# Attention with half-row score products and four score banks

## The reference, cut to what matters

```
q = (seq2 + b_self) @ Wq + bq          # 128 x 128, as 16 heads of 8
k = concat(seq1 + b_prev, seq2 + b_self) @ Wk + bk
v = concat(seq1, seq2) @ Wv + bv
score_prev = einsum('bhqd,bhkd->bhqk', q, k[:, :, :l1]) * SCALE
score_self = (q * k[:, :, l1:]).sum(-1) * SCALE
weights = softmax(concat(where(mask, score_prev, -inf), score_self))
attn = weights[..., :-1] @ v[:, :, :l1] + weights[..., -1:] * v[:, :, l1:]
out = attn @ Wo + bo
```

## Time and profile before

| what | value |
|---|---|
| time, median of 3 runs | 452.58 us (448.89 to 454.62) |
| span of the profiled execution | 429.2 us |
| attention's steps with scores (i = 2 to 17) | 10.0 to 158.4 us of the span |
| PE busy share of the span | 87% |
| DVE, ACT, POOL | 65%, 58%, 46% |
| TensorE's granted clock, mean | 0.942 of full |

### The profile page before, as it was taken

The page is one execution under the profiler, slowest core; times in us unless marked ns, Lnnn a source line. Parts: engine busy times, 40 slices in busy tenths (PEclk is TensorE's granted clock), DMA queues, the critical chain, the costliest instruction groups (busy, mean ns, idle before and its releaser), DMA issues.

```text
span 429.2 us, 10202 instructions
## 1 busy us (share of the span) xinstructions
PE 375.2 (87%) x2637; PEld 270.4 (63%) x2637; DVE 278.9 (65%) x1132; ACT 247.4 (58%) x743; POOL 197.5 (46%) x273
## 2 busy tenths in 40 slices
PE   4999999899999995799998998479988779899960
PEld 4456556556666652689998997145565457677650
DVE  4566888888878888376555666369566536365562
ACT  2688788788887891546555564328874124344420
POOL 5421254444334434544554555223737506466561
PEclk9999999999999996599999999569999999899995
DMA  7603999678888404467767675320101122232354
GB/s 150 95 15 97 391 279 251 165 166 199 195 204 182 89 20 136 113 160 180 215 165 199 173 175 155 106 94 21 57 26 52 48 52 72 69 79 76 81 172 147
DMA packets 61072, 57.14 MB, mean 133 GB/s; under 512 B 6042, under 2 KB 49703, under 8 KB 60768
## 3 DMA queue, kind: packets, MB, share of 16 engines
q1 hardware_dynamic: 56288, 48.10, 45.1%
q0 software_dynamic: 4736, 8.47, 5.8%
HBM read 36.12 MB, written 21.73 MB: 135 GB/s over the span
## 4 chain that ended last, share of the span: by engine, by line
PE 58%; issue 12%; DMA 9%; DVE 8%; POOL 6%; ACT 4%; SPq 1%; POOLq 1%; DVEq 0%; ACTq 0%
PE bank L764 13%; PE bank L773 6%; PE bank L896 5%; PE bank L787 5%; PE bank L901 5%; DMA layer_outputs<-w_all 3%; POOL layer_outputs L744 3%; PE bank L1023 3%; DMA w_all<-layer_rows 2%; POOL layer_outputs L702 2%; PE bank L1103 2%; DMA qexp<-layer_outputs 2%; PE bank L804 2%; PE bank L818 2%; PE bank L871 2%
## 5 line engine op out<-in xcount | busy, mean ns | idle before, releaser
L1151 ACT ACTIVATE ps<-bank,ntop 128x128 f32<-128x128 f32 x256 | 73.4, 378 | 11.8 <-DVE ntop L1414 10.1
L1218 ACT ACTIVATE hT<-bank,w 128x128 f32<-128x128 f32 x176 | 50.8, 368 | 40.4 <-PE bank L896 40.1
L764 PE MATMUL bank<-qexp 128*128 128x512 f32 x128 | 67.8, 612 | 0.5 <-ACT ps L1151 0.5
L744 POOL DMA_INDIRECT layer_outputs<-w_all x40 | 39.9, 997 | 39.1 <-DVE w_all L1917 21.7
L773 PEld LDWEIGHTS bank<-ident,ps 128*128 128x128 f32 x256 | 31.9, 141 | 33.3 <-issue 29.8
L896 PE MATMUL bank<-xT,w 128*128 128x128 f32 x352 | 49.1, 284 | 2.8 <-DMA w<-in_L_ffn_w_dram 1.2
L1160 ACT ACTIVATE pT<-bank 128x512 f32<-128x512 f32 x64 | 38.6, 603 | 19.1 <-PE bank L773 18.1
L1413 DVE TENSOR_REDUCE mx<-bank 128x4 f32<-128x512 f32 x64 | 43.7, 683 | 8.5 <-PE bank L764 7.0
L668 POOL TENSOR_TENSOR qexp<-kA,rowmask 128x512 f32<-128x512 f32 x15 | 15.6, 1037 | 69.1 <-DVE kA L1498 69.1
L896 PEld LDWEIGHTS bank<-xT,w 128*128 128x128 f32 x352 | 44.6, 199 | 4.0 <-issue 2.6
L732 POOL DMA_INDIRECT layer_rows<-rows_all,places x32 | 30.8, 961 | 24.7 <-DVE rows_all L1791 10.3
(11 more groups left out here) (328 smaller groups left out, 814.6 us busy)
## 6 DMA issues: line engine op xcount, KB each, us to landing
w<-in_L_ffn_w_dram SPq DMA_DIRECT2D x44, 258.0 KB, 3.4
layer_rows<-fill SPq DMA_DIRECT2D x10, 910.0 KB, 9.1
w_all<-in_L_ffn_w_dram SPq DMA_DIRECT2D x24, 256.0 KB, 4.7
qexp<-layer_outputs SPq DMA_DIRECT2D x8, 512.0 KB, 4.0
xt<-layer_rows SPq DMA_DIRECT2D x45, 65.0 KB
w_all<-layer_rows SPq DMA_DIRECT2D x40, 65.0 KB, 1.9
xfT<-in_xfT_dram SPq DMA_DIRECT2D x16, 128.0 KB, 2.4
layer_rows<-fill SPq DMA_DIRECT2D x1, 1560.0 KB, 12.3
```

Source lines behind the costliest of these rows:

```text
L744: g.indirect_dma_start(ys1_dram, bass.IndirectOffsetOnAxis(ap=xt1[r][:, P:P + 1].bitcast(U32), axis=0), yb1[r][:, :], None, bounds_check=Y ...
L764: pe.matmul(psA[g % 2][:, :], qexp[b % 2][:, g, :], kexp[b % 2].rearrange("p g k -> p (g k)"), start=True, stop=True).then_inc(a_in_ps, 1)
L1151: m = s.activation(ps[g % 2][:, t, :], psA[g % 2][:, t * P:(t + 1) * P], ACT.Exp, bias=ntop[:, h:h + 1])
L1218: s.activation(hT[r % 2][:, c, :], banks[c][:, 0:P], ACT.Gelu, bias=w1[r][:, F0 + c:F0 + c + 1]).then_inc(gelu_done, 1)
```

## The change

- A head's eight rows of q and k now lie so that the groups' rows fall into halves: `rowmask` (four columns) is folded into `halfmask` (two columns), and `kexp` holds 2 x 128 columns, not 4 x 128.
- A score product uses 64 rows. `scores(b, pair)` issues four products of 256 columns: for each of two j, one with rows 0 to 63 into bank `2*pair` and one with rows 64 to 127 into bank `2*pair+1`. Two calls per item take the place of four.
- There are four score banks, one for each group. The turned weights go back into the bank from which their scores came; `psT` is gone.
- Waits: scores of a pair wait for the copies of the turned weights of the item before (`pT_ready`), no longer for exponentials (`exp_done`).
- PE's order in step i becomes: scores(i-2,0), turned(i-3,2), L804's product, values(i-3,1), turned(i-3,3), values(i-3,2), L818 to L843's products, turned(i-2,0), L858's product, values(i-3,3), scores(i-2,1), turned(i-2,1), L871 to L876's products, values(i-2,0).
- ACT's order becomes: weights(i-3,3), kept(i-3,2), ws, v, weights(i-2,0), kept(i-3,3), qb, weights(i-2,1), oT, attT, kept(i-2,0), kept(i-2,1), weights(i-2,2). DVE's and POOL's orders stay.
- The columns of Wv, Wo and bv are laid out on the host in another order to match.

```diff
-        kexp = [t[:, 3 * NJ:4 * NJ, :] for t in qexp]
+        kexp = [t[:, 3 * NJ:3 * NJ + NG // 2, :] for t in qexp]
...
-        psT = banks[0:2]
-        psA = banks[2:4]
+        psA = banks[0:4]
...
-                    g.tensor_tensor(kexp[b % 2], kA[:, :].unsqueeze(1).broadcast_to([P, NG, P]),
-                                    rowmask[:, :].unsqueeze(2).broadcast_to([P, NG, P]), ALU.mult).then_inc(kexp_ready, 1)
+                    g.tensor_tensor(kexp[b % 2], kA[:, :].unsqueeze(1).broadcast_to([P, NG // 2, P]),
+                                    halfmask[:, :].unsqueeze(2).broadcast_to([P, NG // 2, P]), ALU.mult).then_inc(kexp_ready, 1)
...
-            def scores(b, g):
+            def scores(b, pair):
...
-                atleast(pe, exp_done, 4 * b + (g - 1))
-                pe.matmul(psA[g % 2][:, :], qexp[b % 2][:, g, :], kexp[b % 2].rearrange("p g k -> p (g k)"), start=True, stop=True).then_inc(a_in_ps, 1)
+                atleast(pe, pT_ready, 4 * (b - 1) + (2 * pair + 2))
+                for j in range(2):
+                    for half in range(2):
+                        at = slice(half * (P // 2), (half + 1) * (P // 2))
+                        m = pe.matmul(psA[2 * pair + half][:, 2 * P * j:2 * P * (j + 1)], qexp[b % 2][at, 2 * pair + j, :],
+                                      kexp[b % 2][at, :, :].rearrange("p g k -> p (g k)"), start=True, stop=True)
+                        if j == 1:
+                            m.then_inc(a_in_ps, 1)
...
                 pe.wait_ge(exp_done, 4 * b + (g + 1))
-                atleast(pe, pT_ready, 4 * b + (g - 1))
                 for j in range(NJ):
-                    m = pe.transpose(psT[g % 2][:, j * P:(j + 1) * P], ps[g % 2][:, j, :], ident[:, :])
+                    m = pe.transpose(psA[g][:, j * P:(j + 1) * P], ps[g % 2][:, j, :], ident[:, :])
...
-                s.activation(pT[g % 2][:, :], psT[g % 2][:, :], ACT.Identity).then_inc(pT_ready, 1)
+                s.activation(pT[g % 2][:, :], psA[g][:, :], ACT.Identity).then_inc(pT_ready, 1)
...
-                atleast(dve, exp_done, 4 * b + (g - 1))
+                atleast(dve, exp_done, 4 * (b - 1) + (g + 1))
```

More of the change, by code:

```diff
@@ L137, in attention_moe_kernel @@
         oT = qexp[0][:, 2 * NJ:2 * NJ + 2, :].rearrange("p g q -> p (g q)")
-        kexp = [t[:, 3 * NJ:4 * NJ, :] for t in qexp]
+        kexp = [t[:, 3 * NJ:3 * NJ + NG // 2, :] for t in qexp]
         rowmask = sb("rowmask", [P, NG])
+        halfmask = sb("halfmask", [P, NG // 2])
         mx = sb("mx", [P, H])
@@ L428, in attention_moe_kernel @@
         ALL_CONSTS = CONSTS + 32
-        KEYS_MASKED, HEADS_MASKED = 3, 6
+        KEYS_MASKED, HEADS_MASKED = 3, 7
         STEPS = B + 6
@@ L754, in _ @@
             mm_.then_inc(cb_in_ps, 1)
-            def scores(b, g):
+            def scores(b, pair):
                 if not 0 <= b < B:
                     return
-                if g == 0:
+                if pair == 0:
                     pe.wait_ge(qexp_pool, b + 1)
                     pe.wait_ge(kexp_ready, b + 1)
-                atleast(pe, exp_done, 4 * b + (g - 1))
-                pe.matmul(psA[g % 2][:, :], qexp[b % 2][:, g, :], kexp[b % 2].rearrange("p g k -> p (g k)"), start=True, stop=True).then_inc(a_in_ps, 1)
+                atleast(pe, pT_ready, 4 * (b - 1) + (2 * pair + 2))
[6 more added lines that the diff above has]
+                            m.then_inc(a_in_ps, 1)
             def turned_weights(b, g):
@@ L796, in _ @@
                 turned_weights(i - 3, 2)
-                weighted_values(i - 3, 1)
                 if active(i, 1):
@@ L804, in _ @@
                     pe.matmul(ps_v1[:, :, 0:DH], new[:, 0:P], wv.rearrange("d (h c) -> d h c", c=DH), start=True, stop=True).then_inc(z_in_ps, 1)
-                scores(i - 2, 1)
+                weighted_values(i - 3, 1)
                 turned_weights(i - 3, 3)
@@ L845, in _ @@
                     m.then_inc(kqv_in_ps, 1)
-                scores(i - 2, 2)
                 turned_weights(i - 2, 0)
-                weighted_values(i - 3, 3)
                 if active(i, 4):
@@ L858, in _ @@
                     pe.transpose(ps_att, att[i % 2][:, :], ident[:, :]).then_inc(att_in_ps, 1)
-                scores(i - 2, 3)
+                weighted_values(i - 3, 3)
+                scores(i - 2, 1)
                 turned_weights(i - 2, 1)
-                weighted_values(i - 2, 0)
                 m = None
@@ L878, in _ @@
                     m.then_inc(mid_in_ps, 1)
+                weighted_values(i - 2, 0)
             pe.wait_ge(v_ready, B)
@@ L1150, in weights @@
                     h = place(g, t)
-                    m = s.activation(ps[g % 2][:, t, :], psA[g % 2][:, t * P:(t + 1) * P], ACT.Exp, bias=ntop[:, h:h + 1])
+                    m = s.activation(ps[g % 2][:, t, :], psA[g][:, t * P:(t + 1) * P], ACT.Exp, bias=ntop[:, h:h + 1])
                 m.then_inc(exp_done, 1)
@@ L1159, in keep_turned @@
                 atleast(act, pv_done, 4 * b + (g - 1))
-                s.activation(pT[g % 2][:, :], psT[g % 2][:, :], ACT.Identity).then_inc(pT_ready, 1)
+                s.activation(pT[g % 2][:, :], psA[g][:, :], ACT.Identity).then_inc(pT_ready, 1)
             for i in range(1, STEPS):
                 weights(i - 3, 3)
+                keep_turned(i - 3, 2)
                 if active(i, 3):
@@ L1168, in _ @@
                     s.activation(ws[(i - 3) % 2][:, :], sm[:, :], ACT.Exp).then_inc(ws_ready, 1)
-                keep_turned(i - 3, 2)
-                weights(i - 2, 0)
                 if active(i, 1):
@@ L1179, in _ @@
                     s.activation(v32[(i - 1) % 3][:, :, 0:VW], ps_v1, ACT.Identity, scale=keymask[:, i - 1:i]).then_inc(v_ready, 1)
+                weights(i - 2, 0)
                 keep_turned(i - 3, 3)
-                weights(i - 2, 1)
                 if active(i, 1):
@@ L1190, in _ @@
                     s.activation(qb[:, :], ps_q, ACT.Identity, bias=cbias[:, 2:3]).then_inc(qb_ready, 1)
-                keep_turned(i - 2, 0)
+                weights(i - 2, 1)
                 if active(i, 3):
@@ L1203, in _ @@
                     s.activation(attT[i % 2][:, :], ps_att, ACT.Identity, bias=bv_col).then_inc(attT_ready, 1)
+                keep_turned(i - 2, 0)
+                keep_turned(i - 2, 1)
                 weights(i - 2, 2)
-                keep_turned(i - 2, 1)
             act.wait_ge(chain_l, 5 * B)
@@ L1363, in _ @@
             dve.wait_ge(pool_const, FIRST_CONSTS)
-            v.tensor_copy(ind_order[:, :].rearrange("p (a t g) -> p t a g", a=2, g=2), ind[:, :].rearrange("p (t a g) -> p t a g", a=2, g=2)).then_inc(dve_const, 1)
+            v.tensor_copy(ind_order[:, :].rearrange("p (j g a) -> p j g a", g=2, a=2), ind[:, :].rearrange("p (a g j) -> p j g a", a=2, g=2)).then_inc(dve_const, 1)
             dve.wait_ge(w_att, 16 * 2)
@@ L1370, in _ @@
             cc.link(v.tensor_reduce(rowmask[:, :], ind[:, :].rearrange("p (g j) -> p g j", g=NG), AX_X, ALU.add))
-            v.tensor_scalar(rowmask[:, :], rowmask[:, :], 0.0, None, ALU.is_gt).then_inc(rows_masked, 1)
+            cc.link(v.tensor_tensor(halfmask[:, :], rowmask[:, 0:NG // 2], rowmask[:, NG // 2:], ALU.add))
+            v.tensor_scalar(halfmask[:, :], halfmask[:, :], 0.0, None, ALU.is_gt).then_inc(rows_masked, 1)
             def valid_keys(b):
@@ L1407, in below_maximum @@
                 ofg = lambda t: t[:, :].rearrange("p (a t o) -> p a o t", a=2, t=NG)[:, g // 2, g % 2, :]
-                view = psA[g % 2][:, :].rearrange("p (t k) -> p t k", t=NG)
+                view = psA[g][:, :].rearrange("p (t k) -> p t k", t=NG)
                 if g == 0:
@@ L1525, in _ @@
                     dve.wait_ge(kA_ready, 1)
-                    v.tensor_tensor(kexp[0], kA[:, :].unsqueeze(1).broadcast_to([P, NG, P]),
-                                    rowmask[:, :].unsqueeze(2).broadcast_to([P, NG, P]), ALU.mult).then_inc(kexp_ready, 1)
+                    v.tensor_tensor(kexp[0], kA[:, :].unsqueeze(1).broadcast_to([P, NG // 2, P]),
+                                    halfmask[:, :].unsqueeze(2).broadcast_to([P, NG // 2, P]), ALU.mult).then_inc(kexp_ready, 1)
                 below_maximum(i - 2, 2)
@@ L1953 @@
     every = lambda name: _np.broadcast_to(laid[name].reshape(1, -1), (P, laid[name].size))
-    grouped = lambda w: w.reshape(-1, NG, 2, 2, DH).transpose(0, 2, 1, 3, 4).reshape(-1, P)
+    grouped = lambda w: w.reshape(-1, 2, 2, NJ, DH).transpose(0, 3, 2, 1, 4).reshape(-1, P)
     laid["xfT"] = _np.concatenate([laid["x"].transpose(0, 2, 1), laid["fside_BxSxS_0"].transpose(0, 2, 1)], axis=2)
```

## The result

The changed kernel takes 439.33 us (434.08 to 441.11, four runs) where the kernel before takes 453.56 (448.89 to 454.62): a ratio of 0.9673, 95% interval 0.9582 to 0.9764, or 14.2 us less. The forecast was 439.3.

What follows compares the result with a forecast made beforehand. PE was taken to bound the kernel, busy for all of a 9.36 us step. 14 steps saving 1.06 (14.8 us), plus 1 and 0.5, less 0.8, 1.2 and 1, gave 13.3 off 452.6: 439.3 us, range 433 to 455.

Steps and rivals of the forecast that it cites:

- Half rows side by side: PE's score products: two row halves run together, so a pair of groups takes 1.13 us in place of 1.72.
- C: PE's score pairs: halves overlap only partly, 1.07 for 0.86, steps 8.7 to 8.8 us, 443 to 447 us; chance 0.10.
- D: PE's score pairs: row tiles run one after the other, 1.89 us a pair, step 9.8, 457 to 465 us; chance 0.13.
- The step: One attention step, paced by PE: a sum of 8.11 us plus 0.2 gives 8.3, from 9.36.
- What the shorter step uncovers: Attention stalls: losses of 0.8 us (DVE's step 8), 1.2 (item 6's input), about 1 (ACT and DVE, steps up to 7).
- First and last step: Ends of the attention: the first step, at half clock, gains perhaps 1 us, the shorter last one about 0.5.
- The tight waits: Three PE waits on ACT's results in a step of 8.3 us; none costs anything if ACT keeps up.
- (1): Next item's scores on PE wait for ACT's copy of turned(i-2,1); about 0.9 us of work fits by 0.15.
- (2): PE's L818 waits for v from ACT, ending near 3.1 us into the step against PE's 3.3.
- POOL's shadow on DVE: DVE's 0.71 us ntop instruction waits 0.55 for POOL; halving POOL's key copy saves about 0.5, so the wait may go.
- Rival B: ACT or a wait on it sets the pace: steps near 8.8 to 9.1 us, 444 to 450 us; chance 0.20.
- Time against span: Whole kernel: the same 13.3 us comes off the span, 429.2 to 415.9, and off the time, 452.6 to 439.3.

Runs made afterwards that it cites:

- e3: Changed kernel with a score pair's two loops exchanged, both products of rows 0 to 63 before those of rows 64 to 127: 436.28 us, ratio 0.974 to before.
- e6: Changed kernel with DVE's constants moved from step 8 to step 2 and key masks into steps 1 to 4: 435.46 us, ratio 0.961 to before.
- e4: Changed kernel run again, unchanged: 440.05 us against 452.97 for the kernel before, ratio 0.974.
- e7: From e6, second layer's weights loaded behind items 2 and 3, not in one burst behind item 5: 435.00 us, ratio 0.957 to before.
- e5: Changed kernel with one exchange on ACT, weights(i-2,2) before the copy of turned(i-2,1): 452.08 us, ratio 0.998 to before.
- e2: Changed kernel's half rows and four score banks, with the old order on PE and ACT: 451.31 us, ratio 1.019 to before.
- e1: Kernel before with the four score banks and new PE and ACT order, but full-row products of 512 columns: 446.14 us, ratio 1.000 to before.
- e8: From e7, turned(i-3,3) put before values(i-3,1) on PE: 433.08 us, ratio 0.960 to before.
- e0: Kernel before, unchanged, profiled a second time: 448.92 us, ratio 1.010 to its other runs; span 447.2 us.

## Why the prediction was right

The mechanism is the one forecast, halves side by side with PE as the pace. That the time fell on the forecast to 0.1 us is luck: the step's saving was 4.8 us larger than forecast in all, and other terms took most of it back.

- **Half rows side by side: right.** A pair at 1.06 for the forecast's 1.13; e3 shows that it doesn't depend on the order of issue, which also rules out rivals C and D.
- **The step: 7.96, forecast 8.3.** The sum came to 8.11 and 0.2 was put on top for wider weight loads. That addition failed: where the sum took 1.03, a pair comes to 1.06. And L808 and L870, taken at 0.12 less than before, cost 0.20 less. The term "14 full steps x 1.06" should have been 1.40 each, 4.8 us more.
- **What the shorter step uncovers: too small.** Forecast were 0.8 for step 8's constants, 1.2 for item 6's input and 1 for the steps up to 7. The intervals between the L808 products in which steps 7 to 9 show lasted 9.80, 8.07, 8.40 and 11.43 us, 5.9 over four times 7.96, where before one interval of 10.62 was 1.3 over 9.36. That is 4.6 of new loss, and about 0.5 more lies in steps 3 to 6: 5.1 for the 3.0 forecast. Part of it no term had: after the wait for DVE the clock fell, and 3.4 us at half the clock cost up to 1.7. The causes of both stalls were named rightly: e6 removes the one, e4 names the DMA and e7 removes the wait.
- **First and last step: too large.** Forecast were 1 and 0.5 of gain. From the first profiles, the first scores start 0.23 later and their step is 0.81 shorter, 0.6 together; and from the last item's first scores to the first expert product it takes 23.74 us for 23.29, a loss of 0.45 whose cause stays open. So the sum as measured is 19.6 + 0.6 - 0.45 - 5.1 = 14.7 us, which is how much earlier the first expert product starts, for the 13.3 forecast.
- **The tight waits: right.** e5 prices (1) at 1.24 us a step when the copy stands behind four exponentials, and e2 meets (1) and (2) in the old order, 0.54 and 0.53. In the changed kernel the copy starts at 87.58 as soon as the turn is there, and the next scores at 88.45. That they cost nothing, as the prediction had it for a kept pace of ACT, is owed to ACT's new order.
- **POOL's shadow on DVE: gone, as said, but not by the shorter copy alone.** The ntop instruction that took up to 1.0 us takes 0.166 at most:

```profile
L1412 DVE TENSOR_TENSOR ntop<-mx,nself x64: 162/164/166, 13.1 to 144.3; 128x4 f32<-128x4 f32 x64
```

  In e1, with the new order and the full key copy, its longest is already 0.363, and in e2, with the halved copy and the old order, 0.447. So it shortens with either part of the change. Whether a step of 7.96 would hold with the full copy no run tells.
- **Rival B (ACT as the pace)** didn't come, at 8.8 to 9.1, but e8 shows how near it is: PE from turned(i-3,3) to turned(i-2,1), and ACT from there through one copy and two groups of exponentials to the next turned(i-3,3), form one loop. That it sets the pace with PE is read from the traces' order, not tested by itself; it fits that two changes of shape less on PE move the step by 0.02 us. ACT idles 0.4 us a step, and just there. The Trainium skill's rule on evacuation (TensorEngine Tiling (Array Packing), "PSUM Bottleneck") thus bears out in part, as the next limit and not as this one's: of ACT's share of that loop one instruction is a copy out of PSUM and eight are exponentials that read it.
- **Time against span.** Added to a median of 452.6, the difference was nearly right: 14.2 us measured for 13.3, while the median of before, with one run more, rose by 1.0, which hides the 0.9. The reading that 23 us lie outside the engines' instructions was wrong (e0). It did no harm to the sum, as the part behind the attention was taken as unchanged.

## What to carry to other kernels

Row-halved products pay when the freed time isn't behind a copy that another engine does in its own order: here the half rows alone cost 1 to 2%, the order alone nothing, and both together gain about 3%. Ask of a wait that a change adds which instruction stands ahead of the awaited one on its engine; one pair of lines was worth 1.24 of 1.40 us a step. And when a loop gets shorter, look for the steps in which other engines or the loads had extra work that fitted before, and move that work to where the pipeline is still filling: it gave another 1 to 1.5 per cent.

## What the hardware showed

Products on two halves of the rows ran side by side: 0.86 us for eight instructions of 0.216 each, besides the 0.20 for the change of shape, whichever order they were issued in, the upper half starting 7 ns after the lower where one instruction of the lower half is written between their first ones, and 13 ns where three are. The Trainium skill (TensorE: Matmul & The Clock Gate, "The mechanism") has matmuls start and end in program order throughout; the measurement differs, as in strict order only one stretch of 0.216 of e3's pair would overlap, 1.71 us by its forecast for the 1.07 measured. A change of the array's shape cost 0.15 to 0.20 us each way: 1.91 for 1.72 (e1), 0.59 for 0.44, 0.42 for 0.22. Why the second layer of one profiled execution took 18 us less than that of another with the same program stays open.
